# A four-layer convolution sequence on one Trainium2 core: sampling offsets loaded by GpSimd in one piece for x and y, window rows spread on VectorE, the fourth offset convolution behind the first batch

## What is computed

```python
def deform_conv(x, w, b, ow, ob):
    off = conv2d(x, ow, ob).reshape(Bn, K, 2, Hh, Ww)            # K = 9 taps, an offset in y and x for each
    cy = iy + dy + off[:, :, 0]; cx = ix + dx + off[:, :, 1]
    y0 = floor(cy); x0 = floor(cx); wy = cy - y0; wx = cx - x0
    samp = gather(y0, x0, (1-wy)*(1-wx)) + gather(y0, x0+1, (1-wy)*wx) \
         + gather(y0+1, x0, wy*(1-wx)) + gather(y0+1, x0+1, wy*wx)
    return einsum('bckhw,ock->bohw', samp, w)
h = relu(group_norm1(deform_conv(x, w1, b1, ow1, ob1), g1, be1)) + x
h = relu(group_norm1(deform_conv(h, w2, b2, ow2, ob2), g2, be2)) + h
```

## Time and profile before

| | |
|---|---|
| median of 3 runs | 916.06 us |
| lowest and highest | 909.77 and 919.32 us |
| the profiled execution | 915.41 us, its span 913.5 us |
| TensorE | busy 670.8 us (73% of the span), mean granted clock 0.877 |
| VectorE | busy 573.8 us (63%) |
| ScalarE | busy 466.1 us (51%) |
| GpSimd | busy 299.3 us (33%) |
| DMA | 108.7 MB, on average 119 GB/s |

### The profile page before, as it was taken

How to read it: one execution, slowest core, us unless ns; L and a number is a source line. 1 busy time by engine, 2 the same in 40 slices (tenths; PEclk the granted TensorE clock), 3 DMA queues, 4 the chain that set the end, 5 groups by cost and what they waited for, 6 DMA issues and landing times.

```text
span 913.5 us, 30136 instructions
## 1 busy us (share of the span) xinstructions
PE 670.8 (73%) x13944; PEld 467.2 (51%) x13944; DVE 573.8 (63%) x699; ACT 466.1 (51%) x623; POOL 299.3 (33%) x183
## 2 busy tenths in 40 slices
PE   2409999999987677868778378677697778809483
PEld 1104555567854455557556354356485566607252
DVE  6894062221343987868787544788787889477365
ACT  3505433432333657867777141486876787532413
POOL 6000000000033185967673005137776766000000
PEclk9758999999998897989999779879889989958687
DMA  4000000000069989899995009989999989000002
GB/s 153 0 0 1 3 4 2 3 17 4 17 166 231 252 210 213 216 220 202 202 194 132 2 3 240 246 236 228 218 209 216 202 214 199 4 1 4 1 4 93
DMA packets 27752, 108.70 MB, mean 119 GB/s; under 512 B 6004, under 2 KB 10740, under 8 KB 19432
## 3 DMA queue, kind: packets, MB, share of 16 engines
q1 hardware_dynamic: 24488, 96.26, 44.6%
q0 software_dynamic: 3136, 10.49, 4.8%
HBM read 91.84 MB, written 19.65 MB: 122 GB/s over the span
## 4 chain that ended last, share of the span: by engine, by line
PE 40%; DVE 25%; DMA 18%; ACT 7%; issue 6%; SPq 3%; DVEq 0%; ACTq 0%
DMA arena<-offsets_by_batch 17%; PE psum L1234 13%; PE psum L1281 10%; PE psum L1210 5%; DVE arena L744 4%; DVE arena L743 4%; DVE arena L742 4%; PE psum L1428 3%; PE psum L1316 3%; SPq L489 3%; PE psum L1339 2%; ACT arena L1080 2%; PE psum L1293 2%; PE psum L1435 1%; PE psum L1247 1%
## 5 line engine op out<-in xcount | busy, mean ns | idle before, releaser
L1316 PE MATMUL psum<-arena 64*64 64x198 f32 (+4 forms) x4512 | 251.7, 371 | 74.4 <-issue 32.8
L417 POOL TENSOR_SCALAR arena<-arena 128x384 f32<-128x384 f32 (+2 forms) x124 | 250.6, 2041 | 165.3 <-PE psum L1316 161.8
L1316 PEld LDWEIGHTS psum<-arena 64*64 64x64 f32 x4512 | 199.0, 149 | 127.6 <-issue 81.0
L742 DVE SCALAR_TENSOR_TENSOR arena<-arena 128x792 f32<-128x792 f32 (+3 forms) x96 | 96.2, 1002 | 67.7 <-ACT arena L1080 67.5
L1079 ACT ACTIVATE arena<-arena 128x792 f32<-128x792 f32 (+3 forms) x96 | 84.7, 882 | 78.5 <-DMA arena<-offsets_by_batch 78.4
L1234 PE MATMUL psum<-arena 32*32 32x512 f32 x3456 | 115.0, 597 | 0.3 <-DVE arena L666 0.3
L1281 PE MATMUL psum<-arena 32*32 32x512 f32 x2304 | 90.3, 668 | 31.4 <-issue 25.6
L1484 POOL DMA_DIRECT2D columns<-arena x16 | 10.0, 753 | 299.5 <-DVE arena L708 242.9
L744 DVE SCALAR_TENSOR_TENSOR arena<-arena 128x792 f32<-128x792 f32 (+3 forms) x96 | 100.5, 1047 | 0.0
L743 DVE SCALAR_TENSOR_TENSOR arena<-arena 128x792 f32<-128x792 f32 (+3 forms) x96 | 98.3, 1024 | 0.0
L1234 PEld LDWEIGHTS psum<-arena 32*32 32x32 f32 x3456 | 73.4, 103 | 39.9 <-issue 13.0
(11 more groups left out here) (137 smaller groups left out, 651.3 us busy)
## 6 DMA issues: line engine op xcount, KB each, us to landing
arena<-offsets_by_batch SPq DMA_DIRECT2D x112, 576.0 KB, 9.6
arena<-offsets_by_batch SPq DMA_DIRECT2D x16, 624.0 KB, 10.8
offsets<-arena SPq DMA_DIRECT2D x32, 256.0 KB, 11.2
offsets_by_batch<-offsets SPq DMA_DIRECT2D x92, 48.0 KB, 10.8
columns<-arena POOLq DMA_DIRECT2D x8, 320.0 KB, 6.7
arena<-columns POOLq DMA_DIRECT2D x8, 320.0 KB, 9.0
arena<-in_x SPq DMA_DIRECT2D x4, 512.0 KB, 5.2
out<-arena SPq DMA_DIRECT2D x8, 256.0 KB, 2.2
```

What stands on the lines that cost most here:

```text
L417: return eng.tensor_scalar(ap(z_at(a, 0) + i * C, [[64, NBK], [ZROW, b - a], [1, C]]), ap(ZC + c % 2 * ZCS + (a - CHUNKS[c][0]) * C, [[ZCB ...
L742: v.scalar_tensor_tensor(term(0), term(0), 0.0, part(tx), ALU.min, ALU.mult)
L1316: ins = t_.matmul(ps_t(s, bank + r, first * K * w, many * K * w), window, ap(g_at(unit, d0) + first * TW + s * w, [[GS + TW, many], [SLOTS ...
```

## The change

1. `load_batch` moves from SP to GpSimd. `offsets_by_batch` now holds x and y of a batch behind each other, so that one transfer brings both. The four transfers of a batch are now of 32 partitions x 18,432 bytes, and their sources have a leading dimension of size 8 where it was 16. The order is partitions 0 to 31, 64 to 95, 32 to 63, 96 to 127. ScalarE waits once for all four.
2. `arrange_batch` issues each of its transfers for x and y apart (6 where it were 3, with a leading dimension of 8 where it was 16), counts on four semaphores in turns, and runs up to four batches ahead of the loads.
3. All four spreads of all batches are on VectorE. From batch 2 on they stand behind the batch's first unit.
4. `convolve(3)` stands behind batch 0 on TensorE, its copy behind unit 2 on ScalarE, and `reach(3)` and `bound_offsets(3)` (now in place, in RAW) behind batch 1 on VectorE.

```diff
-            return IN + (n % 2 * 2 + axis) * INS
+            return IN + n % 2 * 2 * INS + axis * in_rows(n) * W
...
+                if n >= 4:
+                    sp.wait_ge(s_u, NB * L + n - 3)
+                elif L == 1:
+                    sp.wait_ge(s_u, NB)
...
-                    sp.dma_start(bass.AP(batch_d.tensor, n * INS + at, [[NB * INS, 2 * B], [step, 3], [1, rows * W]]),
-                                 bass.AP(off_d.tensor, 3 * (ky + 1) * N + row * W,
-                                         [[KP * N, 2 * B], [N, 3], [1, rows * W]])).then_inc(s_ar[n % 2], 16)
+                    for axis in range(2):
+                        sp.dma_start(bass.AP(batch_d.tensor, (2 * n * ER + axis * in_rows(n)) * W + at,
+                                             [[2 * NB * INS, B], [step, 3], [1, rows * W]]),
+                                     bass.AP(off_d.tensor, (axis * B * KP + 3 * (ky + 1)) * N + row * W,
+                                             [[KP * N, B], [N, 3], [1, rows * W]])).then_inc(s_ar[n % 4], 16)
...
-                if m >= 2:
-                    dve.wait_ge(s_ds[m - 2], 64 * (L + 1))
-                raw, d1 = RAW + m % 2 * NATS, D1 + m % 2 * NATS
+                if m == 2:
+                    dve.wait_ge(s_ds[0], 64 * (L + 1))
+                if m == 3:
+                    dve.wait_ge(s_red, 4 * L + 4)
+                raw, d1 = RAW + m % 2 * NATS, bounded_at(m)
...
                     v.scalar_tensor_tensor(term(2), part(ty), 0.0, part(tx), ALU.min, ALU.mult).then_inc(s_g, 1)
+                    if u == 0 and n >= 2:
+                        spread_windows(L, n)
...
-                for a, b in parts:
-                    for i in (2, 3):
+                for a, b in parts:
+                    for i in range(4):
...
                     batch(L, n)
-                    if n == 0:
+                    if n == 1:
+                        reach(L, 3)
                         bound_offsets(L, 3)
-                        reach(L, 3)
...
-                for unit in range(RING - 1):
+                for unit in range(RING):
                     y_terms(L, unit)
-                copy_offsets(L, 3)
-                y_terms(L, RING - 1)
...
                     if unit + RING < UNITS:
                         y_terms(L, unit + RING)
+                    if unit == NU - 1:
+                        copy_offsets(L, 3)
...
-                convolve(3)
-                pe.wait_ge(s_cve, 16 * (L + 1))
                 pe.wait_ge(s_ws, 16)
                 for unit in range(UNITS):
+                    if unit == NU:
+                        pe.wait_ge(s_cve, 16 * L + 12)
+                        convolve(3)
                     sample(unit)
...
+            def load_batch(L, n):
+
+
+                pool.wait_ge(s_ar[n % 4], arranged(L, n))
+                if n >= 2:
+                    pool.wait_ge(s_g, UNITS * L + NU * (n - 1))
+                for half in range(2):
+                    for r in range(2):
+                        g.dma_start(cols(in_at(n, 0), 2 * in_rows(n) * W, 64 * r + 32 * half, 32),
+                                    bass.AP(batch_d.tensor, 2 * (4 * r * NB + n) * INS,
+                                            [[0, QW // 2], [2 * NB * INS, 4], [1, 2 * in_rows(n) * W]])
+                                    ).then_inc(s_in[n % 2], 16)
...
                 load_windows(L, 0)
+                load_batch(L, 0)
                 load_windows(L, 1)
+                load_batch(L, 1)
                 for n in range(NB):
-                    spread_windows(L, n)
-                    if n in (3, 7):
-                        load_windows(L, (n + 1) // 4 + 1)
+                    if n >= 2:
+                        load_batch(L, n)
+                    if n in (4, 8):
+                        load_windows(L, n // 4 + 1)
```

More of the change, by code:

```diff
@@ L208, in build, with bounded_at @@
         assert 8 * CH <= SPAR and 2 * NATS <= min(N, SPAR)
+        def bounded_at(m):
+            return RAW + NATS if m == 3 else D1 + m % 2 * NATS
         PROJ = T_PAD[3] + PADN - 2 * CH
@@ L213, in build @@
         off_d = nc.dram_tensor("offsets", [2, B * KP, H, W], F32, kind="Internal").ap()
-        batch_d = nc.dram_tensor("offsets_by_batch", [2, B, NB, INS], F32, kind="Internal").ap()
+        batch_d = nc.dram_tensor("offsets_by_batch", [B, NB, 2 * INS], F32, kind="Internal").ap()
         flag_d = nc.dram_tensor("reach", [P, 8], F32, kind="Internal").ap()
@@ L274, in build @@
         s_ds = [sem(f"bounded_offsets_stored_{m}") for m in range(4)]
-        s_inx = [sem("even_x_offsets_loaded"), sem("odd_x_offsets_loaded")]
-        s_iny = [sem("even_y_offsets_loaded"), sem("odd_y_offsets_loaded")]
-        s_ar = [sem("even_offsets_arranged"), sem("odd_offsets_arranged")]
+        s_in = [sem("even_offsets_loaded"), sem("odd_offsets_loaded")]
+        s_ar = [sem(f"offsets_arranged_{i}_of_four") for i in range(4)]
         s_u, s_nd, s_g = sem("offset_distances_ready"), sem("y_terms_ready"), sem("tent_products_ready")
@@ L299, in conv_bank @@
         def conv_bank(m):
-            return 4 if m % 2 == 0 else 0
+            return 0 if m == 1 else 4
         HALF = N // 2
@@ L480, in arrange_batch @@
                     taps(1, KR * W, W, H - 1, 1)
-            def load_batch(L, n):
-                sp.wait_ge(s_ar[n % 2], arranged(L, n))
-                if n >= 2:
-                    sp.wait_ge(s_g, UNITS * L + NU * (n - 1))
-                for axis, done in ((0, s_inx[n % 2]), (1, s_iny[n % 2])):
-                    for r in range(2):
-                        sp.dma_start(cols(in_at(n, axis), in_rows(n) * W, 64 * r, 64),
-                                     bass.AP(batch_d.tensor, (axis * B + 4 * r) * NB * INS + n * INS,
-                                             [[0, QW], [NB * INS, 4], [1, in_rows(n) * W]])).then_inc(done, 16)
             sp.wait_ge(s_c1, NCH * NT)
@@ L722, in reach @@
             def reach(L, m):
+                dve.wait_ge(s_cve, 16 * L + 4 * m + 4)
                 ins = v.tensor_reduce(cols(FM + m * 32, 32), ap(RAW + m % 2 * NATS, [[W, 32], [1, W]]), AX.X, ALU.max,
@@ L1123, in _ @@
                     if unit == 2 * NU:
-                        for m in range(4):
+                        for m in range(3):
                             act.wait_ge(s_ds[m], 64 * (L + 1))
+                        act.wait_ge(s_red, 4 * L + 3)
+                    if unit == 4 * 2 * NU:
+                        act.wait_ge(s_ds[3], 64 * (L + 1))
                         act.wait_ge(s_red, 4 * (L + 1))
@@ L1460, in _ @@
             g.memset(cols(W_OUT, NGRP * Q), 0.0).then_inc(s_woz, 1)
-            def spread_windows(L, n):
-                c, parts = window_rows(n)
-                pool.wait_ge(s_zc[c % 2], 128 * L + 64 * (c // 2 + 1))
-                if n >= 2:
-                    pool.wait_ge(s_un, UNITS * L + NU * (n - 1))
-                elif n < SHARED and L == 1:
-                    pool.wait_ge(s_un, UNITS * L)
-                for a, b in parts:
-                    for i in range(2 if n < SHARED else 4):
-                        ins = spread_part(g, c, a, b, i)
-                ins.then_inc(s_zx, 1)
             def store_columns(L, part):
@@ L1493, in load_windows @@
                 else:
-                    pool.wait_ge(s_zx, NB * L + 4 * (c - 1))
+                    pool.wait_ge(s_zv, NB * L + 4 * (c - 1))
                 first, end = CHUNKS[c]
```

29 lines of the change are left out of this document (10 added, 19 removed).

## The result

| | before | after |
|---|---|---|
| median of the timed runs, us | 917.7 | 933.5 |
| ratio, 95% interval | | 1.019 [1.015, 1.024] |
| span of the profiled execution, us | 913.5 | 934.9 |
| batches 4 to 15 of L = 0, L = 1, us | 153.0, 151.3 | 160.2, 156.6 |

What follows compares the result with a forecast made beforehand. The double-buffered loop of offset loads, with the DMA engines full, was taken to bound the kernel. Layer sums of -6.3 and -7.7 us, together -14.0, took 915.4 to 901 us; range 870 to 932.

Steps and rivals of the forecast that it cites:

- 2.7 + 5.8 + 0.6 + 0.5 + 0.6 = 10.2: Products done to load landed (L), us: fixed part, data at 405 GB/s, second eight engines, stalled issue, arranging.
- The second eight engines start one issue later: 0.6: In each batch's offset load, the second group of eight DMA engines was to start 0.6 us after the first.
- The stalled issue: GpSimd's load issue, held while VectorE's L736 runs, was to add between 0 and 1.4 us, taken as 0.5.
- Bounds: Limits on the time from products done to load landed: 8.0 to 12.0 us around the forecast 10.2.
- The loop: Double buffer: two batches take L + a + b (products done to landing, to first product, to last); 11.7 us a batch.
- a + b: Landing to first product (a, forecast 4.0 us) plus first to last product of a batch (b, forecast 9.2 us).
- the bound: Rival: with the load at its lower end 8.0, VectorE's own 10.6 us a batch sets the pace; 875 us, chance 0.15.
- the ring: Rival: TensorE and ScalarE hold the ring of four units, a batch stays at 12.3 us; 915 us, chance 0.10.
- Batch 3: Batch 3 of each layer, which waited for a load before, was to take 10.6 us: gain 3.5 and 3.4.
- then the convolution 10.8, ScalarE's copies 2.4: Layer start: after TensorE's last unit, these give offsets at 324.9 in L = 0; start losses 5.2 and 2.0 us.
- The loads do not run side by side: Rival: transfers share engines or use all 16, data take 10.3 us again, 14.0 us a batch; 956 us, chance 0.15.
- all small costs at their upper end: Rival: products done to load landed takes 12.0 us, a batch 12.6; 923 us, chance 0.15.

Runs made afterwards that it cites:

- convolution 3 back: The kernel after with the fourth offset convolution, its copies and its bounding at their old places: 912.6 us, 0.993 of before.
- shared rows odd: The kernel after with VectorE's addition of shared rows moved from behind the even batches to behind the odd ones: 933.3 us, 1.018 of before.
- no tent: The kernel after without VectorE's tent of x (L731), so weights are wrong: 923.1 us in one run, 12 batches 156.3 and 152.1 us.
- the kernel in which they truly don't: The kernel after with each batch's loads as two transfers of 64 partitions over sixteen engines instead of four of 32: 970.9 us in a single run.

## Why the prediction was wrong

Between the sum of -14.0 and the +21.4 lie 35.4 us. Of these 26.7 are in batches 4 to 15, where L was put too short, and 9.1 in the two starts.

**The terms of L.** "2.7 + 5.8 + 0.6 + 0.5 + 0.6 = 10.2" against load 14, typical of the waited-for ones:

| | predicted | measured |
|---|---|---|
| products' end to the first landing | 2.7 + 0.5 + 2.9 = 6.1 | 0.60 + 1.18 + 4.49 = 6.3 |
| to the second group's first landing | 0.6 | 2.4 |
| its second transfer | 2.9 + 0.6 for arranging | 4.1 |
| L | 10.2 | 12.8 |

Over the eight even loads without columns beside them (6, 10, 12 and 14 of both layers) the mean L is 12.5: 6.5 to the first landing, 2.2 to the second group's and 3.8 for its second transfer. Loads 4 and 8, with the columns, take 14.0 in the mean.

The first line held, though by two errors: GpSimd begins its issue 0.60 us after the products end (SyncE did so 0.1 us after, as a row of before has it, against 688.51), which no term had; the stall was 0.65 where I took 0.5; the rest was shorter.

```profile
688.58 2.45 SPq L489 DMA_DIRECT2D arena<-offsets_by_batch  x4
```

**"The second eight engines start one issue later: 0.6"** is the step that failed in the batches: the second group lands 2.2 us behind the first in the mean of the eight loads, and that is 1.6 of the 2.3 us by which L was too short. Windows of one microsecond during load 14:

```profile
480.00:481.00 1.00, 1.00 (x36) 0.93 (x32) 1.00 (x2) 0.00 (x0) 0.61 (x2) 1.00 0.45 147
481.00:482.00 1.00, 1.00 (x28) 0.92 (x23) 1.00 (x3) 0.99 (x2) 0.00 (x0) 1.00 1.43 295
...
484.00:485.00 1.00, 1.00 (x24) 0.73 (x20) 1.00 (x2) 0.69 (x2) 0.00 (x0) 1.00 1.09 461
...
487.00:488.00 1.00, 1.00 (x28) 0.68 (x20) 1.00 (x2) 0.00 (x0) 0.00 (x0) 1.00 0.37 147
488.00:489.00 1.00, 0.13 (x8) 0.00 (x0) 0.18 (x1) 0.00 (x0) 0.22 (x1) 1.00 0.05 18
489.00:490.00 1.00, 0.00 (x0) 0.00 (x0) 0.00 (x0) 0.00 (x0) 1.00 (x3) 1.00 0.01 0
```

Eight engines work alone at first and eight alone at the end; full rate stands only between. In the packet records the first eight begin at 479.73 to 479.81, the others from 481.22 on, 1.5 us later and not 0.6, and eight packets there take 1.95 to 2.16 us instead of 0.69. A sum of bytes over the full rate is a lower bound where the parts start apart. Why the second group begins so late, and why its first packets are slow, no run tested.

**The last transfer** holds the other loss of load 14. Its engines but one are through at 488.3; that one carried a packet of program code, 16 KB in 0.98 us, at 486.82, and ends at 489.6; the load lands at 490.05, after two windows with hardly a byte. The DMA view of 477 to 492 counts them:

```profile
q8 instruction: 2, 0.03, 0.8%
```

In four kernels with these transfers (after, convolution 3 back, shared rows odd, no tent) I took the loads of batches 3 to 15 without 4 and 8, 88 in all. In 31 of them such a packet stands right ahead of the packets of the engine that ends last, or between the last data and the landing: they land 12.0 us after their issue and 2.7 us after the third transfer. The other 57 take 10.9 and 1.8, but in 15 of these an engine or the landing is late too, and the records name nothing for it. That is an observation over many loads; no run took the code packets away, so how much of the difference they cause stays open.

**The stalled issue** was seen rightly and, with its bounds 0 to 1.4, sized nearly so: 1.18 for the first issue in most waited-for loads. At batch 2 it was 2.10 (behind the last spread and the tent):

```profile
307.97 3.69 POOL L1496 DMA_DIRECT2D arena<-offsets_by_batch  x4 [22.22 <-DVE arena L739]
```

The Trainium skill (SBUF — State Buffer, section "SBUF: two separate sides") names this stall. By the run without the tent the trace agrees: 0.53 us without the tent beside the issue, 1.18 with it, 0.7 us a pair.

**Bounds.** L was held to lie within 8.0 and 12.0, and 12.0 was 923 us. The even loads were above that end in the mean. The bounds were made from single terms of rows of before; none was there for GpSimd's start 0.6 us behind the products, nor for the two groups drifting apart.

**The sum for the batches.** With the measured L the prediction's own formula gives (13.3 + 4.0 + 9.2)/2 = 13.25 and (12.7 + 13.2)/2 = 12.95, that is 159 and 155 us for twelve, and 160.2 and 156.6 were measured. The loop was the right model. Before, twelve batches in 153.0 and 151.3 us with a + b = 10.5 make L 15.0 and 14.7; so a pair saved 1.7 to 2.0 us in L and paid 2.1 in a and 0.6 in b. VectorE was not the bound and the ring did not hold.

**Batch 3** came as said, 10.55 and 10.54 us for 10.6.

**The start.** The second step that failed is "then the convolution 10.8, ScalarE's copies 2.4". `reach` in L = 0 was to begin at 324.9 and began at 327.20. The convolution took 12.4 us there but ended at 322.3, as the sum has it (322.5); ScalarE's order made the 2.3 us: the y terms of batch 2, which wait for a load that landed at 320.96, stand ahead of the copies. In L = 1 `reach` came far later:

```profile
628.26 2.29 DVE L719 TENSOR_REDUCE arena<-arena 128x32 f32<-128x2048 f32 x1 [12.40 <-ACT arena L1057]
```

TensorE's timeline there, convolution 3:

```profile
610.18 5.47 PE L1280 MATMUL psum<-arena 32*32 32x512 f32 x151
617.67 4.49 PE L1280 MATMUL psum<-arena 32*32 32x512 f32 x128 [2.02 <-issue]
625.80 1.68 PE L1280 MATMUL psum<-arena 32*32 32x512 f32 x9 [3.64 <-issue]
```

It took 17.3 us and stood twice with nothing that the profile can name but its own issue. I had taken 10.8 us from one of the quietest. In the trace of before the last convolution of L = 1 takes 21.2 us, with gaps of the same kind; there nobody waited for it:

```profile
570.59 4.59 PE L1281 MATMUL psum<-arena 32*32 32x512 f32 x128 [1.74 <-issue]
579.65 5.85 PE L1281 MATMUL psum<-arena 32*32 32x512 f32 x128 [4.47 <-issue]
588.62 5.92 PE L1281 MATMUL psum<-arena 32*32 32x512 f32 x120 [3.11 <-issue]
```

The packet records name what the views don't. Two gaps in a row lie 128 matmuls apart, and the packets of program code of 16 KB that ended at 616.24 and 624.42 came 1.4 us before the matmuls of after went on at 617.67 and 625.80. In the traces of all kernels here TensorE stands for more than 0.7 us 85 times within the offset convolutions or between two of them, and each time it goes on 1.2 to 1.7 us after such a packet has ended. So TensorE waits for its code. Why the code came late is not shown: the packets share the engines with the loads, but no run moved either. The term should have been 10.8 to 21.

**The rivals.** "The loads do not run side by side" did not come: 1 us windows at 461 GB/s, and the kernel in which they truly don't takes 971 us. The rule of the Trainium skill (DMA: Bandwidth & Descriptors, "Rules for kernel authors") that transfers to disjoint halves serialize gives as its reason that both use all sixteen engines. For transfers of eight engines issued by GpSimd, to which that reason does not apply, they did not serialize: same bytes, L of 13.0 against 14.7 in the mean of the even batches. Nearest was "all small costs at their upper end", with costs that it did not contain.

## What to carry to other kernels

- In a double-buffered loop write 2T = L + a + b and count what each edit does to all three. Here twice the rate took some 2 us a pair from L, and by the formula the joined transfer and the spreads gave 2.7 back; undoing the joining alone turned +2% into -3%.
- Time a load from "last reader done" to "last byte landed" over its worst part: start of the issuing engine, first issue, lag of the last group, last packet. Bytes over rate is only its floor. And take the price of work that is newly put on the path from the slowest of its kind in the old trace, where it was slow and hidden.
- Look which batches wait for their load: short steps of the engine that frees the buffer, and foreign transfers, delay the loop where such a load is in flight and are nearly free elsewhere.

## What the runs showed of the hardware

- A DMA engine's packets run at 13.3 GB/s where all sixteen write one half of the partitions, and at 26.9 where eight write each half, or where only eight run. The order of four issues alone was worth 32 us.
- Transfers of 32 partitions from GpSimd go to two groups of eight engines in turns; from SyncE all go to one group (share 0.52, 212 and 221 GB/s).
- GpSimd starts an issue 0.53 to 0.6 us after the products that it waits for have ended, SyncE within 0.1 (row at 688.58).
- A convolution of 288 matmuls took 9.8 to 21.2 us. The difference is mostly idle time of TensorE that the profile puts down to issue; in 85 of 85 such gaps a 16 KB packet of program code had ended 1.2 to 1.7 us before the matmuls went on.
